# Turning u, v and x by f16 products of their split parts, and a new order in the second scan

## The chip, the cores and the metric

The kernel runs on one core of one Trainium2 chip. The metric is the device time of one execution in microseconds; lower is better. The host prepares arrays (transposes, stacking, repeated rows) but does no arithmetic of the layer.

## The reference, cut to what matters

One layer of a small language model on tokens of shape (2, 2048), model width 192:

```python
h = embed(x) * sqrt(192) + position                  # per token: 192 values
u = rmsnorm(layernorm(h)) * norm1_w
z, xBC, dt = split(u @ in_proj_w)                    # 384, 512, 24 columns
xBC = silu(conv4(xBC) + conv_b)                      # causal, 4 taps
state = exp(dt*A) * state + dt * x * B               # scan over 2048 tokens, 24 heads of 16, 64 states
y = (state . C + D*x) * silu(z)
m = y @ out_proj_w                                   # back to 192
v = rmsnorm(m) * norm2_w
m = m + (silu(v @ w_gate) * (v @ w_up)) @ w_down     # width 768
h = h + m
xn = layernorm(h)
w, idx = route(sigmoid(xn @ gate_weight.T))          # 8 experts in 4 groups, 2 groups, then 2 experts
h = h + shared(xn) + sum of the chosen experts(xn)   # width 128 each
```

## The kernel before, in words

The 2048 tokens are worked in 16 chunks of 128 tokens, both sequences of the batch together (NB = 2), so that most tiles are 128 partitions by 256 tokens. A ramp starts chunks 0 and 1, a body runs 14 times (once unrolled, 13 times in a hardware loop), and a finale ends the last two chunks. One pass of the body works on three chunks at once: `p` (embedding, norm 1, input projection, convolution of the chunk two ahead), `f` (scan of the chunk one ahead) and `b` (output projection, MLP and experts of the oldest chunk). On every engine the order of instructions is written out by hand; engines meet only through semaphores, and each engine takes its own list strictly in order. So an instruction that waits holds up all that is listed behind it on its engine.

Matrix products whose left side is a normalised activation use pairs of f16 numbers: a value is the sum of a high f16 part and a low f16 part. The width of 192 is cut into channels 0 to 127 and the last 64. The last 64 are packed so that one 128-partition tile holds low parts in 64 partitions and high parts in the other 64; weights for them (`wt_hi`, `wt_lo`) stand in SBUF twice, once for each half. One product then takes five matmuls (`split_products`, L1457): three with the first 128 channels and two with the packed 64.

Activations are normalised with tokens on partitions and have to be turned so that channels are on partitions. Before the change that is done in f32: `transpose_channels` (L1466) issues four f32 transposes of 128x128 for one turn (two overlap in 64 channels), for `un` (L1488), `vn` (L1715) and `xn` (L1777). Then ScalarE casts the turned values from PSUM to the high parts (`split`, L642, two instructions) and VectorE subtracts to get the low parts (`split`, L999, two instructions). Only then can the products start.

The part of the body that matters most is the second scan, the scan of sequence 1 of chunk `f`. VectorE's list there (L1437 to L1450) is: `norm2` (add the MLP's result, statistics), `steps_dt` (three small operations for dt of chunk `p`), `masks` 8 and 9, `norm2_apply` (xn, two instructions), `masks` 10 and 11, `from_state` (state's part of y times the decays), `split_x`, `scanned`, `new_state`. A mask (L1115) multiplies a 128x512 tile of exponentials by the masked products of B and C. GpSimd computes 1/sqrt(var) for xn in between (`rsqrt`, L447) and multiplies the scan's state by its decay (`decayed`, L483) as soon as xn is turned (L620). TensorE's list (`second_scan`, L1657, then `experts`, L1821) is: masked 6 and 7, exponents 10, state read, exponents 11, x projection tiles 0 and 1, masked 8 and 9, turn of xn, x projection tiles 2 and 3, masked 10 and 11, then `state_share` (L1695), which overwrites the PSUM bank that `from_state` reads and so waits for it, then the router and the experts.

The first scan (sequence 0) has the same form; there `turn_v` (L1715) comes between `exponents` 6 and `masked` 4, and the MLP's first product waits for v's split.

At the start SyncE issues the loads. Weights go to `w_raw` with one DMA of 128 partitions and to `wt_raw` with two DMAs of 64 partitions, once for the input projection and once for the rest (L340 to L366). GpSimd's `middle_weights` (L576) waits for all of the rest, VectorE's `middle_weights` (L984) waits for GpSimd, and the first masks stand behind it.

Of the kernel before, what the change touches and what calls it, by code (L numbers as in the profile page):

```python
# [29 lines left out]
NB = 2  # L30
# [71 lines left out]
def program(nc, tokens, position, vocab_ids, table, weights, norms, conv_w, conv_b, shared_rows, d_skip, w_out, w_down,  # L102
            w2, identity, lower_ones, triangle_rows, exponent_rows, pair_rows, spread_rows, out):
    with ExitStack() as ctx:
# [3 lines left out]
        def sem(name):  # L108
# [30 lines left out]
        idf = sb("idf", [128, 128])  # L139
        upper = sb("upper", [128, 128])  # L140
# [14 lines left out]
        un = sb("un", [128, NB, D])  # L155
# [47 lines left out]
        vn = sb("vn", [128, NB, D])  # L203
# [10 lines left out]
        xn = sb("xn", [128, NB, D])  # L214
        x_h = sb("x_h", [128, 2, NB * Q], F16)
# [45 lines left out]
        un_ready, ut_done, u_hi_ready, u_hi_tail, u_lo_ready, u_lo_tail = (sem(n) for n in (  # L261
            "un_ready", "ut_done", "u_hi_ready", "u_hi_tail", "u_lo_ready", "u_lo_tail"))
# [32 lines left out]
        m_out, hm_ready, rm_ready, vn_ready, vt_done = (sem(n) for n in (  # L295
            "m_out", "hm_ready", "rm_ready", "vn_ready", "vt_done"))
        v_hi_ready, v_hi_tail, v_lo_ready, v_lo_tail = (sem(n) for n in (
            "v_hi_ready", "v_hi_tail", "v_lo_ready", "v_lo_tail"))
        gu_done, sg_ready, gt_ready = sem("gu_done"), sem("sg_ready"), sem("gt_ready")
        mlp_done, h1_ready, stat2_ready, r2_ready, xnt_done = (sem(n) for n in (  # L300
            "mlp_done", "h1_ready", "stat2_ready", "r2_ready", "xnt_done"))
        xn_ready = [sem(f"xn_ready{b}") for b in range(NB)]
        x_hi_ready, x_hi_tail, x_lo_ready, x_lo_tail = (sem(n) for n in (
            "x_hi_ready", "x_hi_tail", "x_lo_ready", "x_lo_tail"))
# [34 lines left out]
        def _(sp):  # L339
            def load_weights():  # L340

                part = slice(0, COL_G)
                sp.dma_start(w_raw[:, part], weights[0:DH, part]).then_inc(in_w, 16)
                sp.dma_start(wt_raw[0:DT, part], weights[DH:D, part]).then_inc(in_w, 16)
                sp.dma_start(wt_raw[DT:128, part], weights[DH:D, part]).then_inc(in_w, 16)
                sp.dma_start(nrm[:], norms).then_inc(in_w, 16)
# [90 lines left out]
        def _(pool):  # L437
# [121 lines left out]
            def finale(a, b):  # L559
                weighted_x(b, 0)  # L560
                mixed(a)
                pool.wait_ge(vt_done, a + 1)
# [13 lines left out]
            def middle_weights():  # L576
                m = slice(COL_G, COL_E)
                pool.wait_ge(in_w, 64)
                pool.wait_ge(in_mid, 48)
# [26 lines left out]
            def body(p, f, b):  # L606
# [4 lines left out]
                if f is not None:  # L611
                    pool.wait_ge(vt_done, b + 1)
                    decayed(f, 0)
                    keep(f)
                    gate(f, 0)
# [14 lines left out]
        def _(act):  # L630

            act.wait_ge(in_w, 64)
# [5 lines left out]
            act.wait_ge(in_first, 48)  # L638
            for k in range(KT):
                act.activation(skip[:, k], idf[:], ACT.Copy, scale=dsk[:, k:k + 1]).then_inc(setup_a, 1)  # L640

            def split(c, done, src, hi, taken, head, tail):  # L642

                act.wait_ge(done, c + 1)
                if later(c):
                    act.wait_ge(taken[0], c * taken[1])
                act.copy(hi[:, 0, :], src[:, 0:NB * Q]).then_inc(head, 1)
                act.copy(hi[DT:128, 1, :], src[DT:128, NB * Q:2 * NB * Q]).then_inc(tail, 1)
# [109 lines left out]
            def mixed_norm(c, src=p_out[0]):  # L758
                act.wait_ge(rm_ready, c + 1)
                if later(c):  # L760
                    act.wait_ge(vt_done, c)
                for b in range(NB):
                    ins = act.activation(vn[:, b, :], src[:, b * D:(b + 1) * D], ACT.Copy, scale=rm[:, b:b + 1])
                ins.then_inc(vn_ready, 1)

            def swiglu(c, p):
                for f in range(NF):
# [8 lines left out]
                    if f == 4 and p is not None:  # L776
# [9 lines left out]

            def pre_split(c, src=p_misc):
                split(c, ut_done, src, u_h, (z_done[0], 1), u_hi_ready, u_hi_tail)
# [52 lines left out]
            def finale(a, b):  # L841
# [24 lines left out]
                split(b, vt_done, p_y, v_h, (gu_done, NF), v_hi_ready, v_hi_tail)  # L866
# [12 lines left out]
                split(b, xnt_done, p_y, x_h, (h13_done, NX), x_hi_ready, x_hi_tail)  # L879
# [6 lines left out]
            def split_v(b):  # L886
                split(b, vt_done, p_out[1], v_h, (gu_done, NF), v_hi_ready, v_hi_tail)

            def split_x(b):
                split(b, xnt_done, p_out[1], x_h, (h13_done, NX), x_hi_ready, x_hi_tail)  # L890

            def ramp():
                pre_split(0)
                softplus(0)
                for i in range(2):
                    convolved_in(0, i, p_d)
                    first_tap(0, i)
# [50 lines left out]
        def _(ve):  # L948
# [26 lines left out]
            def setup_first():  # L975

                ve.wait_ge(in_w, 64)
                ve.wait_ge(w_in_hi, 2)
                ve.scalar_tensor_tensor(w_lo[:, 0:COL_G], w_raw[:, 0:COL_G], nrm[:, 0:1], w_hi[:, 0:COL_G],
                                        ALU.mult, ALU.subtract).then_inc(w_in_lo, 1)  # L980
                ve.scalar_tensor_tensor(wt_lo[:, 0:COL_G], wt_raw[:, 0:COL_G], nrm[:, 1:2], wt_hi[:, 0:COL_G],
# [17 lines left out]
            def split(c, head, tail, src, hi, lo, lo_ready, lo_tail):  # L999


                ve.wait_ge(head, c + 1)
                ve.wait_ge(tail, c + 1)
# [19 lines left out]
            def pre_stats(c):  # L1023
                ve.wait_ge(h0_ready, c + 1)
                pre_steps.start()
# [9 lines left out]
                ve.bn_aggr(mv[:, 1, :], stat[:, 1, :]).then_inc(stat_ready, 1)  # L1035

            def pre_apply(c):
                ve.wait_ge(r0_ready, c + 1)
                if later(c):
                    ve.wait_ge(ut_done, c)  # L1040
                ve.tensor_scalar(un[:, 0, :], h0_next[:, 0, :], mv[:, 0, 0:1], r0[:, 0:1], ALU.subtract, ALU.mult)
                ve.tensor_scalar(un[:, 1, :], h0_next[:, 1, :], mv[:, 1, 0:1], r0[:, 1:2], ALU.subtract, ALU.mult)\
                    .then_inc(un_ready, 1)

            def pre_split(c, src=p_misc):
                split(c, u_hi_ready, u_hi_tail, src, u_h, u_l, u_lo_ready, u_lo_tail)
# [96 lines left out]
            def mixed(c, src=p_out[0]):  # L1143

                ve.wait_ge(vn_ready, c + 1)
# [6 lines left out]
            def swiglu(c, p, f):  # L1152
                for t in range(NF):

                    ve.wait_ge(sg_ready, c * NF + t + 1)
                    if t == 0:
# [3 lines left out]
                        .then_inc(gt_ready, 1)  # L1160
                    if f is not None and t in (0, 3):
                        masks(f, (6 + t // 3,))
                    if p is not None:
# [3 lines left out]
                        if t == 2:  # L1167
                            pre_apply(p)
                        if t == 4:
                            pre_split(p)  # L1170
# [27 lines left out]
            def norm2_apply(c):  # L1198
                ve.wait_ge(r2_ready, c + 1)
                if later(c):  # L1200
                    ve.wait_ge(xnt_done, c)
                for b in range(NB):
                    ve.tensor_scalar(xn[:, b, :], h1[:, b, :], mv2[:, b, 0:1], r2[:, b:b + 1], ALU.subtract, ALU.mult)\
                        .then_inc(xn_ready[b], 1)
# [109 lines left out]
            def finale(a, b):  # L1314
                masks(b, range(4))
                from_state(b, 0)
                masks(b, (4, 5))
# [21 lines left out]
                hidden(a, 4, p_gu_a)  # L1339
                mixed(b, p_misc)  # L1340
                split(b, v_hi_ready, v_hi_tail, p_y, v_h, v_l, v_lo_ready, v_lo_tail)
# [10 lines left out]
                split(b, x_hi_ready, x_hi_tail, p_y, x_h, x_l, x_lo_ready, x_lo_tail)  # L1352
# [21 lines left out]

            def split_v(b):
                split(b, v_hi_ready, v_hi_tail, p_out[1], v_h, v_l, v_lo_ready, v_lo_tail)

            def split_x(b):
                split(b, x_hi_ready, x_hi_tail, p_out[1], x_h, x_l, x_lo_ready, x_lo_tail)

            def ramp():
# [4 lines left out]
                pre_apply(0)  # L1386
                pre_onehot(1)
                setup_first()
                pre_split(0)
# [4 lines left out]
                pre_apply(1)  # L1394
                for m in range(NM):
                    for k in range(1, KC):
                        convolve_tap(0, m, k)
                operands(0)
                pre_split(1, p_out[1])
# [24 lines left out]
            def body(p, f, b):  # L1424
                if f is not None:
                    masks(f, range(4))
                    from_state(f, 0)
                    masks(f, (4, 5))
# [8 lines left out]
                norm2(b)  # L1437
                if p is not None:
# [17 lines left out]
        def _(pe):  # L1456
# [31 lines left out]
            def pre_turn(c, dst=p_misc):  # L1488
# [591 lines left out]
```

## Time and profile before

| | us |
|---|---|
| median of 3 runs | 842.77 |
| lowest, highest | 842.55, 845.16 |
| the profiled execution's own time | 844.69 |
| its span | 842.9 |

Busy time over the span: PE (TensorE) 794.4 us (94%), DVE (VectorE) 652.8 us (77%), ACT (ScalarE) 538.5 us (64%), POOL (GpSimd) 305.0 us (36%). The page's slices show PE at nine tenths or more from the fifth slice of 40 to the last but one, and a granted TensorE clock of nine tenths or more in all but three of them, which lie in the ramp. Of the chain that ended last, 59% is PE, 17% DVE. The busy share of an engine is an average; which wait ends last is read for each stage from the timeline, which gives the start and the length of each instruction (a row with xN merges N alike; PE's lengths overlap, so for PE the distance of starts counts).

### The profile page before, as it was taken

Reading aid. Unit: us, or ns where it says so; the run is one execution under the profiler, and the core shown is the slowest. Engines: PE = TensorE matmul, PEld = TensorE weight load, DVE = VectorE, ACT = ScalarE, POOL = GpSimd, SP = SyncE. Lnnn points to the kernel's source line nnn. Section 1 sums busy time; section 2 is a strip of 40 time slices with the busy share of each in tenths; the row PEclk is TensorE's granted clock in tenths of the full one; section 3 lists DMA queues with packets and bytes.
Section 4 is the critical chain, followed back from the end, with each engine's and each line's share of the span. In section 5 each row is a group of like instructions: output and inputs, shape, how many; then the busy total and the mean of one; then the engine's idle time right before and its main releaser. Section 6 shows DMA issues by size and latency. Waiting matters only on the chain.

```text
span 842.9 us, 23062 instructions
## 1 busy us (share of the span) xinstructions
PE 794.4 (94%) x7310; PEld 659.0 (78%) x7310; DVE 652.8 (77%) x1680; ACT 538.5 (64%) x1208; POOL 305.0 (36%) x445
## 2 busy tenths in 40 slices
PE   3558999999999999999999999999999999999997
PEld 2435787878888787888878787887878788787786
DVE  5786987977778797877879787787878778787645
ACT  4735575766767576776757667675767767575433
POOL 3552242343424235342423434342343434233222
PEclk9887999999999999999999999999999999999999
DMA  7600000000000000000000000000000000000000
GB/s 252 185 2 14 1 7 20 5 21 0 23 0 5 17 4 19 0 23 0 5 17 5 17 0 23 0 5 17 5 17 0 23 0 5 17 5 10 2 1 19
DMA packets 17107, 16.77 MB, mean 20 GB/s; under 512 B 6322, under 2 KB 15416, under 8 KB 16824
## 3 DMA queue, kind: packets, MB, share of 16 engines
q1 hardware_dynamic: 17080, 16.43, 6.8%
q8 instruction: 15, 0.25, 0.1%
q14 instruction: 12, 0.10, 0.0%
HBM read 12.23 MB, written 4.19 MB: 19 GB/s over the span
## 4 chain that ended last, share of the span: by engine, by line
PE 59%; DVE 17%; issue 11%; POOL 6%; DMA 3%; ACT 2%; DVEq 1%; SPq 1%; POOLq 0%; ACTq 0%
PE bank L1463 24%; PE bank L1744 7%; PE bank L1631 7%; DVE xa L1058 5%; POOL w_raw L555 5%; PE bank L1620 4%; PE bank L1817 4%; PE bank L1700 3%; PE bank L1691 3%; DVE mr L1115 2%; DVE w_raw L1371 2%; PE bank L1676 2%; DMA wt_raw<-weights 2%; DVE w_raw L1284 1%; PE bank L1469 1%
## 5 line engine op out<-in xcount | busy, mean ns | idle before, releaser
L744 ACT ACTIVATE er<-bank 128x512 f32<-128x512 f32 x192 | 109.4, 596 | 57.2 <-PE bank L1620 56.6
L1115 DVE SCALAR_TENSOR_TENSOR mr<-er,gm 128x512 f32<-128x512 f32 x192 | 134.3, 734 | 15.0 <-ACT er L744 14.8
L1817 PE MATMUL bank<-w2t,w_raw 128*128 128x192 f32 x576 | 112.4, 326 | 0.0
L1058 DVE SCALAR_TENSOR_TENSOR xa<-xr,cw_,xa 128x256 f32<-128x256 f32 x192 | 92.8, 492 | 8.8 <-ACT xa L664 7.2
L815 ACT ACTIVATE sg<-bank 128x256 f32<-128x256 f32 x144 | 55.0, 382 | 63.3 <-PE bank L1463 52.4
L1817 PEld LDWEIGHTS bank<-w2t,w_raw 128*128 128x128 f32 x576 | 91.0, 190 | 1.1
L775 ACT ACTIVATE sg<-bank 128x256 f32<-128x256 f32 x90 | 34.5, 383 | 89.3 <-PE bank L1463 89.3
L1631 PE MATMUL bank<-mr,xd 128*32 128x128 f32 x1536 | 71.9, 285 | 15.4 <-DVE mr L1115 14.8
L1463 PE MATMUL bank<-x_h,w_lo 128*128 128x256 f16 x288 | 78.9, 274 | 0.0
L1463 PE MATMUL bank<-x_h,wt_lo 128*128 128x256 f16 x288 | 78.9, 274 | 0.0
L1463 PE MATMUL bank<-x_l,w_hi 128*128 128x256 f16 x288 | 78.9, 274 | 0.0
L1463 PE MATMUL bank<-x_h,wt_hi 128*128 128x256 f16 x288 | 78.9, 274 | 0.0
L1463 PE MATMUL bank<-x_h,w_hi 128*128 128x256 f16 x288 | 78.8, 274 | 0.0
L1744 PE MATMUL bank<-wd,gt 128*128 128x192 f32 x384 | 73.7, 327 | 0.6 <-DVE gt L1159 0.6
L1284 DVE TENSOR_TENSOR w_raw<-sg,bank 128x256 f32<-128x256 f32 x144 | 60.0, 416 | 14.5 <-ACT sg L815 13.6
L451 POOL TENSOR_SCALAR var<-mv 128x2 f32<-128x2 f32 x32 | 6.9, 216 | 175.7 <-DVE mv L1192 127.9
L555 POOL TENSOR_TENSOR w_raw<-w_raw 128x384 f32<-128x384 f32 x64 | 63.9, 998 | 14.6 <-ACT w_raw L803 8.3
L1620 PE MATMUL bank<-ri,lj 128*128 128x512 f16 x192 | 66.6, 385 | 2.6 <-DMA ri<-sums 2.3
L1631 PEld LDWEIGHTS bank<-mr,xd 128*32 128x32 f32 x1536 | 36.2, 110 | 37.1 <-DVE mr L1115 24.1
L1371 DVE SCALAR_TENSOR_TENSOR w_raw<-bank,cw,w_raw 128x192 f32<-128x192 f32 x128 | 47.5, 413 | 19.1 <-POOL w_raw L555 15.4
L1744 PEld LDWEIGHTS bank<-wd,gt 128*128 128x128 f32 x384 | 60.8, 190 | 1.8 <-DVE gt L1159 1.2
L1463 PE MATMUL bank<-v_h,w_hi 128*128 128x256 f16 x192 | 52.3, 273 | 0.8 <-DVE gt L1159 0.3
(240 smaller groups left out, 2169.4 us busy)
## 6 DMA issues: line engine op xcount, KB each, us to landing
out<-w_raw SPq DMA_DIRECT2D x16, 192.0 KB, 2.0
w_raw<-weights SPq DMA_DIRECT2D x1, 1924.0 KB, 10.5
wt_raw<-weights SPq DMA_DIRECT2D x2, 962.0 KB, 15.9
pos<-position SPq DMA_DIRECT2D x16, 96.0 KB, 2.8
ri<-exponent_rows SPq DMA_DIRECT2D x4, 384.0 KB, 4.7
tok<-tokens SPq DMA_DIRECT2D x16, 70.0 KB
sums<-lj SPq DMA_DIRECT2D x16, 64.0 KB, 2.2
ri<-sums SPq DMA_DIRECT2D x64, 12.0 KB
```

What stands on the lines that cost most here:

```text
L555: pool.tensor_tensor(acc[:], acc[:], wt_out[:, e % NWT], ALU.add).then_inc(acc_done, 1)
L744: act.activation(er[:, r % NER], p_d[r % 2][:].rearrange("p (h i) -> p h i", h=HG), ACT.Exp)\
L815: act.activation(sg[:, e % 4, :], src[e][:, 0:NB * Q], ACT.Silu).then_inc(sx_ready, 1)
L1058: ve.scalar_tensor_tensor(xa[:, m], xr[:, m, :, k:k + Q], cw_[:, m, k:k + 1], xa[:, m], ALU.mult, ALU.add)\
L1115: ve.scalar_tensor_tensor(mr[:, r % NER], er[:, r % NER], 1.0, gm[:, r // NQ, :].unsqueeze(1).to_broadcast([128, HG, Q]), ALU.min, ALU.mult)\
L1284: ve.tensor_tensor(hh[:, e % NHH, :], sg[:, e % 4, :], src[e][:, NB * Q:2 * NB * Q], ALU.mult)\
L1371: ins = ve.scalar_tensor_tensor(acc[:, b], p_ex[e][:, b * D:(b + 1) * D], cw[:, b, e - 1:e], acc[:, b], ALU.mult, ALU.add)
L1463: ins = pe.matmul(out_, a, b, start=(i == 0), stop=(i == len(parts) - 1))
L1620: pe.matmul(p_d[r % 2][:].rearrange("p (h i) -> p h i", h=HG), lj[:, b, f, :], ri[:, b, f, of, :], start=True, stop=True).then_inc(d_done, 1)
L1631: ins = pe.matmul(p_y[row:row + 32, k * Q:(k + 1) * Q], xd[:, b, h, :], mr[:, r % NER, heads.index(h), :], start=False, stop=(h % 2 == 1), ...
L1744: ins = pe.matmul(dst[:, b * D:(b + 1) * D], gt[:, f, b * Q:(b + 1) * Q], wd[:, f, :], start=(f == 0 and b == 0), stop=(f == NF - 1), skip ...
L1817: ins = pe.matmul(p_ex[e][:, b * D:(b + 1) * D], hh[:, e % NHH, b * Q:(b + 1) * Q], w2t[:, e, :], start=True, stop=True)
```

## The change

Normalised values are split into f16 parts while tokens are still on partitions, and the parts are turned by f16 matmuls against an f16 identity. `u_t`, `v_t` and `x_t` hold the two parts of each channel side by side (step of two elements). The last 64 channels with both parts are then 128 adjacent columns, and one matmul turns them into the packed tile; its weights are repeated row by row by the host, so that `wt_raw` is loaded by one DMA of 128 partitions. After the turn ScalarE copies the high tile (one instruction) and VectorE the low tile (one instruction).

- u: VectorE subtracts the mean (`uc`, two instructions), ScalarE scales into the high parts (`pre_high`, two instructions, behind its third Silu), VectorE forms the low parts (`pre_low`, two instructions), TensorE turns behind the MLP's last gate and up products instead of the last but one.
- v: ScalarE's scaling writes the high parts in f16, VectorE forms the low parts from PSUM (`v_low`, between masks 4 and 5), TensorE turns behind `exponents` 7.
- x: VectorE does it all: normalise (two instructions), one f16 copy, one subtraction.

```diff
-                ve.tensor_tensor(lo[:], src[:, 0:NB * Q], hi[:, 0, :], ALU.subtract).then_inc(lo_ready, 1)
-                ve.tensor_tensor(hi[0:DT, 1, :], src[DT:128, NB * Q:2 * NB * Q], hi[DT:128, 1, :], ALU.subtract)\
-                    .then_inc(lo_tail, 1)
+            def low_parts(c, src, scale, parts, ready):
+
+                for b in range(NB):
+                    ins = ve.scalar_tensor_tensor(parts[:, b, :, 1], src[b], scale[:, b:b + 1], parts[:, b, :, 0],
+                                                  ALU.mult, ALU.subtract)
+                ins.then_inc(ready, 1)
+
+            def low_in(c, turned, src, lo, ready):
+                ve.wait_ge(turned, c + 1)
+                ve.tensor_copy(lo[:], src).then_inc(ready, 1)
...
             def norm2_apply(c):
                 ve.wait_ge(r2_ready, c + 1)
...
+                ve.wait_ge(xn_ready, c + 1)
+                ve.tensor_copy(x_t[:, :, :, 0], xn[:]).then_inc(xh_ready, 1)
+                ve.wait_ge(xh_ready, c + 1)
+                ve.tensor_tensor(x_t[:, :, :, 1], xn[:], x_t[:, :, :, 0], ALU.subtract).then_inc(xl_ready, 1)
...
                 norm2(b)
+                if f is not None:
+                    masks(f, (8, 9))
+                norm2_apply(b)
                 if p is not None:
                     steps_dt(p)
                 if f is not None:
-                    masks(f, (8, 9))
-                norm2_apply(b)
-                if f is not None:
                     masks(f, (10, 11))
+                split_x(b)
                 if f is not None:
                     from_state(f, 1)
-                split_x(b)
...
-            def transpose_channels(dst, src, done):
-
+            def turn(c, dst, low, parts, high_ready, low_ready, high_turned, low_turned):
+
+                pe.wait_ge(high_ready, c + 1)
                 for b in range(NB):
-                    pe.transpose(dst[:, b * Q:(b + 1) * Q], src[:, b, 0:DH], idf[:])
+                    pe.matmul(dst[:, b * Q:(b + 1) * Q], parts[:, b, 0:DH, 0], id16[:], start=True, stop=True)
+                pe.wait_ge(low_ready, c + 1)
                 for b in range(NB):
-                    ins = pe.transpose(dst[:, (NB + b) * Q:(NB + b + 1) * Q], src[:, b, D - 128:D], idf[:])
-                ins.then_inc(done, 1)
+                    ins = pe.matmul(dst[:, (NB + b) * Q:(NB + b + 1) * Q], parts[:, b, DH:D, :].rearrange("p c s -> p (c s)"), id16[:],
+                                    start=True, stop=True)
+                ins.then_inc(high_turned, 1)
+                for b in range(NB):
+                    ins = pe.matmul(low[:, b * Q:(b + 1) * Q], parts[:, b, 0:DH, 1], id16[:], start=True, stop=True)
+                ins.then_inc(low_turned, 1)
...
                 skipped_x(1, 1)
                 masked(c, (8, 9))
-                turn()
                 if p is not None:
                     project_in_x(p, p_d, (2, 3), c)
+                turn()
                 skipped_x(1, 2)
                 masked(c, (10, 11))
...
-                    pool.wait_ge(xnt_done, b + 1)
+                    pool.wait_ge(xl_turned, b + 1)
                     decayed(f, 1)
...
                 sp.dma_start(w_raw[:, rest], weights[0:DH, rest]).then_inc(in_mid, 16)
-                sp.dma_start(wt_raw[0:DT, rest], weights[DH:D, rest]).then_inc(in_mid, 16)
-                sp.dma_start(wt_raw[DT:128, rest], weights[DH:D, rest]).then_inc(in_mid, 16)
+                sp.dma_start(wt_raw[:, rest], weights[DH:DH + 128, rest]).then_inc(in_mid, 16)
```

## Rows read from the trace of the kernel before

**Rows 1.** Windows: stretch, then busy us and count of each engine, granted clock, DMA.
```profile
450.00:499.00 49.00, 48.73 (x460) 40.73 (x459) 39.41 (x105) 33.38 (x76) 18.23 (x27) 1.00 0.03 10
```
**Rows 2.** Timeline of PE, turn of u: start, length, line, tiles, shape, count.
```profile
436.48 0.38 PE L1469 MATMUL bank<-idf,un 128*128 128x128 f32 x2
436.70 0.38 PE L1471 MATMUL bank<-idf,un 128*128 128x128 f32 x2
```
**Rows 3.** Timeline of PE, f16 products of 128 columns in the running sums.
```profile
455.14 0.22 PE L1583 MATMUL bank<-triangles,pa 128*128 128x128 f16 x1
...
455.25 0.22 PE L1583 MATMUL bank<-triangles,pa 128*128 128x128 f16 x1
```
**Rows 4.** Timeline of PE, the first scan: exponents 6, turn of v, first v product.
```profile
474.52 0.39 PE L1620 MATMUL bank<-ri,lj 128*128 128x512 f16 x1
474.95 0.43 PE L1469 MATMUL bank<-idf,vn 128*128 128x128 f32 x2
...
477.72 0.27 PE L1463 MATMUL bank<-v_h,w_hi 128*128 128x256 f16 x1
```
**Rows 5.** Timeline of DVE, the second scan.
```profile
442.52 0.21 DVE L1071 TENSOR_TENSOR dx<-bank,shared 128x48 f32<-128x48 f32 x1
...
442.98 1.29 DVE L1115 SCALAR_TENSOR_TENSOR mr<-er,gm 128x512 f32<-128x512 f32 x2
444.25 0.67 DVE L1203 TENSOR_SCALAR xn<-h,mv,r 128x192 f32<-128x192 f32 x2
444.83 1.29 DVE L1115 SCALAR_TENSOR_TENSOR mr<-er,gm 128x512 f32<-128x512 f32 x2
446.04 0.55 DVE L1126 TENSOR_TENSOR t<-bank,ecx 128x384 f32<-128x384 f32 x1
446.57 0.42 DVE L1004 TENSOR_TENSOR x_l<-bank,x_h 128x256 f16<-128x256 f32 x1
```
**Rows 6.** Timeline of PE, the same second scan: state share, then the router.
```profile
447.48 0.91 PE L1700 MATMUL bank<-xw,bt 128*128 128x384 f32 x2
448.23 0.17 PE L1463 MATMUL bank<-w_hi,x_h 128*128 128x8 f16 x1
```
**Rows 7.** Timeline of POOL: second scan (two rows), then the first scan's rsqrt.
```profile
443.11 1.11 POOL L453 TENSOR_TENSOR r<-var,mhalf 128x2 f32<-128x2 f32 x1
445.75 1.07 POOL L490 TENSOR_TENSOR state<-state,ends 128x384 f32<-128x384 f32 x1 [1.53 <-PE bank L1785]
...
472.04 0.61 POOL L503 TENSOR_SCALAR vv<-ss 128x2 f32<-128x2 f32 x1 [2.67 <-ACT junk L755]
472.74 1.04 POOL L505 TENSOR_TENSOR rm<-vv,mhalf 128x2 f32<-128x2 f32 x1
```
**Rows 8.** Timeline of DVE: the masks beside these two; in the ramp, masks 6 and 7.
```profile
470.71 2.50 DVE L1115 SCALAR_TENSOR_TENSOR mr<-er,gm 128x512 f32<-128x512 f32 x4
...
51.92 2.08 DVE L1115 SCALAR_TENSOR_TENSOR mr<-er,gm 128x512 f32<-128x512 f32 x2
```
**Rows 9.** Timeline of POOL, the ramp, beside masks 6 and 7.
```profile
52.08 1.38 POOL L497 TENSOR_TENSOR y<-y,zs 128x384 f32<-128x384 f32 x1 [1.89 <-DVE y L1135]
```
**Rows 10.** Groups of DVE: a cast to 16 bits; count, busy us, mean ns, idle before.
```profile
L966 DVE CAST tab<-tab_rest 70x192 bf16<-70x192 f32 x1 | 0.3, 256 | 0.0
```
**Rows 11.** Chain that ended last, in the ramp: start, length, what.
```profile
13.96 17.70 DMA wt_raw<-weights
31.85 4.17 POOL w_hi L581
...
40.82 0.78 DVE mr L1115
```
**Rows 12.** Timeline of ACT, the ramp: the exponentials of masks 0 and 1.
```profile
36.08 1.08 ACT L744 ACTIVATE er<-bank 128x512 f32<-128x512 f32 x2 [1.45 <-PE bank L1620]
```
**Rows 13.** DMA from 12 to 23 us, then from 23 to 32 us.
```profile
DMA packets 853, 4.06 MB, mean 369 GB/s; under 512 B 103, under 2 KB 192, under 8 KB 695
...
DMA packets 403, 1.58 MB, mean 176 GB/s; under 512 B 304, under 2 KB 304, under 8 KB 304
```

More of the change, by code:

```diff
@@ L630, in _ @@
         def _(act):
-            act.wait_ge(in_w, 64)
+            act.wait_ge(in_first, 48)
+            act.copy(id16[:], idf[:]).then_inc(setup_a, 1)
+            act.wait_ge(in_w, 48)
             act.activation(w_hi[:, 0:COL_G], w_raw[:, 0:COL_G], ACT.Copy, scale=nrm[:, 0:1]).then_inc(w_in_hi, 1)
@@ L637, in _, with set_skip, high_in @@
             act.activation(aexp[:], alog, ACT.Exp).then_inc(setup_a, 1)
[L638 to L644, printed above, removed]
+            def set_skip():
+                for k in range(KT):
+                    act.activation(skip[:, k], idf[:], ACT.Copy, scale=dsk[:, k:k + 1]).then_inc(setup_a, 1)
+            def high_in(c, turned, src, hi, taken, ready):
+                act.wait_ge(turned, c + 1)
                 if later(c):
                     act.wait_ge(taken[0], c * taken[1])
-                act.copy(hi[:, 0, :], src[:, 0:NB * Q]).then_inc(head, 1)
-                act.copy(hi[DT:128, 1, :], src[DT:128, NB * Q:2 * NB * Q]).then_inc(tail, 1)
+                act.copy(hi[:], src[:].rearrange("p (k t) -> p k t", k=2)).then_inc(ready, 1)
             def convolved_in(c, i, src=p_d):
@@ L1035, in pre_stats, with pre_low, pre_split @@
                 ve.bn_aggr(mv[:, 1, :], stat[:, 1, :]).then_inc(stat_ready, 1)
-            def pre_apply(c):
-                ve.wait_ge(r0_ready, c + 1)
[L1039 to L1046, printed above, removed]
+                ve.wait_ge(stat_ready, c + 1)
+                for b in range(NB):
+                    ins = ve.tensor_scalar(uc[:, b, :], h0_next[:, b, :], mv[:, b, 0:1], None, ALU.subtract)
+                ins.then_inc(uc_ready, 1)
+            def pre_low(c):
+                ve.wait_ge(uc_ready, c + 1)
+                ve.wait_ge(r0_ready, c + 1)
+                ve.wait_ge(uh_ready, c + 1)
+                low_parts(c, (uc[:, 0, :], uc[:, 1, :]), r0, u_t, ul_ready)
+            def pre_split(c, src=p_out[1][:, NB * Q:2 * NB * Q]):
+                low_in(c, ul_turned, src, u_l, u_lo_ready)
             def convolve_tap(c, m, k):
@@ L1153, in swiglu @@
                 for t in range(NF):
+                    if p is not None and t == NF - 1:
+                        pre_split(p)
                     ve.wait_ge(sg_ready, c * NF + t + 1)
@@ L1160, in swiglu @@
                         .then_inc(gt_ready, 1)
+                    if p is not None and t == 3:
+                        pre_low(p)
                     if f is not None and t in (0, 3):
@@ L1316, in finale @@
                 from_state(b, 0)
-                masks(b, (4, 5))
+                masks(b, (4,))
+                v_low(a)
+                masks(b, (5,))
                 split_v(a)
@@ L1373, in weighed_sum, with v_low @@
                 ins.then_inc(out_sum, 1)
+            def v_low(c, src=p_out[0]):
+                ve.wait_ge(vh_ready, c + 1)
+                low_parts(c, (src[:, 0:D], src[:, D:2 * D]), rm, v_t, vl_ready)
             def split_v(b):
-                split(b, v_hi_ready, v_hi_tail, p_out[1], v_h, v_l, v_lo_ready, v_lo_tail)
+                low_in(b, vl_turned, p_pair[1][:, 0:NB * Q], v_l, v_lo_ready)
             def split_x(b):
-                split(b, x_hi_ready, x_hi_tail, p_out[1], x_h, x_l, x_lo_ready, x_lo_tail)
+                low_in(b, xl_turned, p_out[0][:, NB * Q:2 * NB * Q], x_l, x_lo_ready)
             def ramp():
@@ L1427, in body @@
                     from_state(f, 0)
-                    masks(f, (4, 5))
+                    masks(f, (4,))
+                v_low(b)
+                if f is not None:
+                    masks(f, (5,))
                 split_v(b)
@@ L1486, in pre_embed, with pre_turn @@
                 ins.then_inc(emb_done, 1)
-            def pre_turn(c, dst=p_misc):
-                pe.wait_ge(un_ready, c + 1)
-                transpose_channels(dst, un, ut_done)
+            def pre_turn(c, dst=p_misc, low=p_out[1][:, NB * Q:2 * NB * Q]):
+                if not later(c):
+                    pe.wait_ge(setup_a, 1)
+                turn(c, dst, low, u_t, uh_ready, ul_ready, uh_turned, ul_turned)
             def project_dt(c, dst=p_out[1]):
@@ L1653, in first_scan @@
                 exponents(c, 7)
+                between()
                 masked(c, (5,))
@@ L1767, in swiglu @@
                         exponents(f_, 9)
-                    if f == 4 and p is not None:
+                    if f == NF - 1 and p is not None:
                         pre_turn(p)
```

165 lines of the change are left out of this document (87 added, 78 removed).

## The prediction, made before the changed kernel was run

> **What bounds the kernel now.** I read the page's busy shares first, then one window of the loop, then PE's timeline, and last the lists of DVE and POOL where PE's next wait could come from. In a 49 us window, about one pass of the body, PE is busy for 48.73 us at full granted clock, DVE for 39.41 [rows 1]. So in the 14 passes a microsecond less of PE stream is a microsecond gained, if nothing else is late. What can be late is seen in the second scan. There `from_state` ends at 446.59 and `state_share`, which needs it, starts at 447.48 [rows 5, 6]: DVE has 0.89 us to spare, no more. The times below are those of this one pass. In the ramp another chain sets the end: weights landing, GpSimd, DVE's masks [rows 11].
>
> **PE's stream.** A turn is four f32 transposes; two pairs start 0.22 us apart, so a turn takes 0.44 us [rows 2]. It becomes six f16 products of 128 columns with a weight load each. Such products stand in the running sums, two starts every 0.11 us, so 0.055 us each [rows 3]: 6 x 0.055 = 0.33 us, 0.11 less a turn. Their stationary side is contiguous there; in four of the six new ones it is strided, which no row shows. Bounds: 0.055 us, and the f32 transpose's 0.11 us, by which a turn costs 0.66. I take the f16 row, since load and product overlap in both. The id16 copy happens once, off the path.
> The Trainium skill, "TensorE: Matmul & The Clock Gate", section "Back-to-back issue gap", gives about 81 ns for a sustained pair of weight load and 128-column product. By it a turn would be 0.49 us, slower than now. The rows here disagree (0.055 us with alternating weights), so I go by them; the rule is a rival below.
>
> **The v side.** PE finishes exponents 6 at about 474.74 (0.22 after its start) and begins v's turn at 474.95: 0.2 us lost waiting. The first v product comes at 477.72, behind ACT's two and DVE's two split operations [rows 4]. After the change the turn stands behind exponents 7 and skipped_x, so the high parts are there. DVE's `v_low` (two operations of 192; nearest row xn's pair, 0.67 us, upper bound 0.85 at x_l's 0.42 each [rows 5]) runs while PE does masked 4. Mask 5 is queued behind it, and masked 5 on PE waits some 0.3 us for it. One copy per engine replaces two, so v's first product no longer waits once `state_share` is issued. Net 0.1 from stream and 0.3 from waits: I take -0.4 us, bounds 0 and -0.5.
>
> **The u side.** PE's stream gives -0.11. DVE gets two subtractions, two `low_parts` and a copy for two `un` operations and two split ones; ACT two scalings and a longer copy for two casts. All stand under the MLP's products, whose `gt` tiles are made a full product group ahead; the turn moves behind the last group, and two groups of `mlp_down` hide u's copies. gt 5 stands behind the u copy on DVE, with the same two groups to hide it. Without this cover the copy's 0.4 us would be lost. I take -0.1, so PE reaches the second scan 0.5 us earlier; DVE and POOL, which follow the MLP's end, move along.
>
> **The second scan.** Now follow DVE. After `norm2`, where dx started at 442.52, masks 8 and 9 stand first: 442.52 - 0.5 = 442.02, ending after 1.29 us [rows 5] at 443.31. They now run while POOL computes r2. What that does is seen in the first scan, where four masks run from 470.71 to 473.21 [rows 8]: `vv` takes 0.61 us for two elements, ending with a mask, and `rm` ends at 473.78, 0.57 us after the last mask [rows 7]. POOL's operation waits for a mask to end. So r2 is done at 443.31 + 0.57 = 443.88 and xn starts at 443.91; before, r2 ended at 443.11 + 1.11 = 444.22 [rows 7], xn started at 444.25. Of the 0.5 us gained, 0.34 is left.
> From xn's start, all in DVE's list: xn 0.67; wait 0.03; the f16 copy of 384; wait 0.03; the subtraction of 384; `steps_dt` 0.46 (442.52 to 442.98); masks 10 and 11, 1.21 (444.83 to 446.04); `split_x`, one copy from PSUM, 0.34 (x_l's 0.42 less an overlap of 0.08); `from_state` 0.55 [rows 5]. The subtraction is priced by `from_state`'s 0.55 for 384, 0.47 to the next start. For the copy only a cast of 192 is there, 0.256 us [rows 10]. Bounds for 384: 0.256 (if width cost nothing) and 0.55. I take 0.36: the cast plus 0.10 for 192 more elements, half of what the f32 operations take for as many (0.55 for 384, some 0.35 for one of xn's 192). Sum: 0.67 + 0.03 + 0.36 + 0.03 + 0.47 + 0.46 + 1.21 + 0.34 + 0.55 = 4.12 us, and `state_share` follows 0.05 later: 443.91 + 4.17 = 448.08. Before, xn's start to the end of `from_state` was 2.34 us.
> PE would come there at 447.48 - 0.5 - 0.11 = 446.87. Thus 0.6 us later than before even when nothing collides.
> Something does collide. POOL's `decayed` for sequence 1 is released by x's turn. The low parts end 0.4 us before mask 10 starts; PE has four products left, so POOL begins while mask 10 runs. Such a case stands in the ramp: POOL's `gate` began at 52.08, 0.16 us into mask 6 [rows 9], and masks 6 and 7 took 2.08 us for 1.29 [rows 8]: mask 7 waited for POOL. Before, `decayed` began at 445.75, in mask 11, which had no mask behind it; it ended 0.7 us after that mask's end [rows 5, 7]. So mask 11 is held for about 0.65 us, bounds 0 and 0.79. `split_x`, `from_state`, `state_share` and on PE everything behind stand in that line: 448.73, or 1.2 us later than before a pass (447.48 to 448.7).
> The delay isn't won back: behind `state_share` PE goes on with router and experts without a gap (448.23 is just when the share's 0.75 us is over [rows 6]). ACT's softplus now waits for dt and stands ahead of its x copy; by the same chain that copy is ready some 0.4 us before the router, so it is nearly late, not late. 14 x 1.2 = +16.8 us.
>
> **The ramp.** The last of the weights land at 13.96 + 17.70 = 31.66; POOL's high parts follow, and the first mask starts at 40.82 [rows 11], though its exponentials were begun at 36.08 [rows 12]. Up to 23 us DMA moves 369 GB/s, after that 176, with 1.58 MB left [rows 13]: the two half-height DMAs run at half speed. Full height at 369 GB/s would take 4.3 us for that, not 9, and land 4.4 us earlier. SP also issues two DMAs fewer, and each queue entry behind them moves up. From 40.82 the mask can move up until its exponentials' end near 36.7. I take -3.5, bounds 0 (if the slow stretch isn't due to the height) and -4.4.
>
> **The finale.** Its masks 10 and 11 get copy and subtraction ahead of them (+0.9), and its splits each lose two short operations (about -0.3 a time). I take 0, give or take 1.
>
> **Sum.** 844.69 + 16.8 - 3.5 = 858.0 for the profiled execution, which stands 1.92 above the median of 842.77; so 856 us as median.
>
> **Rivals.**
> - POOL doesn't hold mask 11 (PE's turn comes so late that `decayed` starts after it). For it: only 0.35 us lie between. Then 0.6 x 14 = 8.4, with -3.5 from the ramp: 848.
> - The other side: the second scan's chain stays inside PE's stream, and PE remains the limit. It decides at `state_share`: xn's start to `from_state`'s end would have to take under 2.9 us (443.91 to 446.87) instead of 4.12, say with r2 not held up by masks (-0.6) and copy and subtraction costing next to nothing. For it: PE is 99% busy, so any cover elsewhere pays. Against it: the row prices. The whole 0.6 a pass is kept: 842.8 - 8.4 - 3.5 = 831.
> - The ramp wins nothing, as the loads share one queue whatever their height: 859.6.
> - The 81 ns pair: u and v lose 0.05 instead of gaining 0.11, so 14 x 0.3 = 4.5 more: 860.5. The timeline speaks against it.
>
> **Chances.** Forecast 0.57 (own range 851 to 862), no hold 0.17 (845 to 851), PE stays the limit 0.12, ramp without gain 0.10, the pair rule 0.04. Differences under 0.3% (2.5 us) can't be told from none. Faster gets the 0.12 and a little of the no-hold case's edge, 0.14; same 0.07, from that case with a larger ramp gain; slower 0.79. The range 844 to 864 leaves out the fast case and a tail of further waits in the experts.
>
> **What would show it.** After: f16 turn products 0.055 us apart; first v product about 0.4 us earlier in its pass; DVE idle for half a microsecond before xn; masks 10 and 11 together near 2 us, with `decayed` beside them; PE waiting over 1.5 us before masked 11 and `state_share`; pass length 50.1 instead of 48.9; weights in by about 27.5 us. A `from_state` that ends before PE gets there would make it all wrong.

## The result, and the profile after

The changed kernel takes 865.1 us (median of 6 runs, 863.47 to 867.57), the one before 842.89 beside it on the same chip: a ratio of 1.0259 (95%: 1.0235 to 1.0284). It is slower, as forecast, but by 22 us and not by 13: 865.1 lies above the forecast's range (844 to 864). Below, spans of the two profiled executions are compared: 865.5 us after, 842.9 before. The mean granted clock of the changed kernel's six executions runs from 0.974 to 0.984; the profiled one has 0.974 and took 867.34 us, so it is one of the two longest.

The chain that ended last has one row in each pass that is easy to follow, the last twelve `mlp_down` products (start, length, what). From one to the next is the length of a pass. In the kernel before:

```profile
438.83 1.95 PE bank L1744 x12
...
487.76 1.95 PE bank L1744 x12
```

So 48.93 us. After, the same view:

```profile
246.28 2.02 PE bank L1789 x12
...
298.03 2.02 PE bank L1789 x12
...
449.31 2.02 PE bank L1789 x12
...
499.75 2.02 PE bank L1789 x12
```

Most passes take 50.4 us, 1.5 more than before; but 246.28 to 298.03 is 51.75, and of the 12 passes between the first such row and the thirteenth three are as long as that (51.75 to 51.79).

**The second scan.** The row called h1 below is the one in which `norm2` adds the MLP's result. In the kernel before it is this one on DVE:

```profile
440.91 0.56 DVE L1179 TENSOR_TENSOR h<-bank,hm 128x384 f32<-128x384 f32 x1 [1.21 <-PE bank L1744]
```

The timeline of DVE after, from h1 on (start, length, line, operation, tiles, shape, count, and in brackets the idle time ahead and what ended it), answers to [rows 5]:

```profile
451.45 0.56 DVE L1205 TENSOR_TENSOR h<-bank,hm 128x384 f32<-128x384 f32 x1 [1.35 <-PE bank L1789]
...
453.14 1.29 DVE L1141 SCALAR_TENSOR_TENSOR mr<-er,gm 128x512 f32<-128x512 f32 x2
455.02 0.67 DVE L1229 TENSOR_SCALAR xn<-h,mv,r 128x192 f32<-128x192 f32 x2 [0.58 <-POOL r L452]
455.73 0.39 DVE L1233 CAST x_t<-xn 128x384 f16<-128x384 f32 x1
456.15 0.59 DVE L1235 TENSOR_TENSOR x_t<-xn,x_t 128x384 f16<-128x384 f32 x1
456.63 0.19 DVE L1097 TENSOR_TENSOR dx<-bank,shared 128x48 f32<-128x48 f32 x1
...
457.07 1.93 DVE L1141 SCALAR_TENSOR_TENSOR mr<-er,gm 128x512 f32<-128x512 f32 x2
458.93 0.41 DVE L1027 CAST x_l<-bank 128x256 f16<-128x256 f32 x1
459.26 0.54 DVE L1152 TENSOR_TENSOR t<-bank,ecx 128x384 f32<-128x384 f32 x1
```

The rows show the list that was forecast, in its order: half a microsecond of idling ahead of xn, copy and subtraction, dt, two masks that take 1.93 us where two take 1.29 above, then `split_x` ahead of `from_state`. Beside it POOL, which answers to [rows 7]; its third row runs inside DVE's 1.93 us:

```profile
453.33 0.56 POOL L450 TENSOR_SCALAR var<-mv 128x2 f32<-128x2 f32 x1 [7.53 <-DVE mv L1218]
453.97 1.02 POOL L452 TENSOR_TENSOR r<-var,mhalf 128x2 f32<-128x2 f32 x1
457.55 0.91 POOL L489 TENSOR_TENSOR state<-state,ends 128x384 f32<-128x384 f32 x1 [2.56 <-PE bank L1520]
```

And PE, which answers to [rows 6]:

```profile
457.82 0.42 PE L1677 MATMUL bank<-mr,xd 128*32 128x128 f32 x8
459.06 0.42 PE L1677 MATMUL bank<-mr,xd 128*32 128x128 f32 x8 [0.82 <-DVE mr L1141]
459.91 0.88 PE L1745 MATMUL bank<-xw,bt 128*128 128x384 f32 x2 [0.42 <-issue]
```

PE waits 0.82 us for mask 11, and 0.42 more ahead of `state_share`, which follows `from_state`'s end (459.26 + 0.54) by 0.11. From h1 to `state_share` it is now 459.91 - 451.45 = 8.46 us; before, 447.48 [rows 6] less 440.91 was 6.57.

**The granted clock** is what no forecast had. In windows of PE in a long pass (stretch, its length, busy us and count, granted clock, DMA share, GB/s):

```profile
254.00:256.00 2.00, 1.13 (x16) 1.00 0.00 0
256.00:258.00 2.00, 1.55 (x12) 0.82 0.00 0
258.00:260.00 2.00, 2.00 (x20) 0.50 0.00 0
260.00:262.00 2.00, 2.00 (x17) 0.83 0.00 0
```

PE is not fully busy in 254 to 258, where it has the same waits as those just seen (0.82 us ahead of masked 11, 0.42 ahead of `state_share`); then the clock falls to 0.50, the lower of its two levels (1.2 GHz), and the mean of the next 2 us is 0.83. The pass is 1.33 us longer than its neighbours.

### The profile page after: what moved, and what is told of

The parts are those of the page before. It is cut to its first block, busy times and chain, and to the rows that moved or that the text cites. A ratio compares the mean times of both kernels' runs of the same rounds, so it can differ in the third digit from the quotient of the medians.

```text
span 865.5 us, 23218 instructions
## 1 busy us (share of the span) xinstructions
PE 798.4 (92%) x7406; PEld 659.0 (76%) x7406; DVE 662.2 (77%) x1728; ACT 541.8 (63%) x1193; POOL 301.7 (35%) x445
## 4 chain that ended last, share of the span: by engine, by line
PE 44%; DVE 26%; issue 15%; POOL 9%; ACT 3%; DVEq 1%; DMA 1%; POOLq 0%; SPq 0%; ACTq 0%
PE bank L1506 20%; PE bank L1789 7%; DVE mr L1141 6%; DVE xa L1084 5%; POOL w_raw L554 5%; PE bank L1858 4%; PE bank L1745 3%; PE bank L1677 3%; DVE w_raw L1405 2%; POOL r L452 2%; PE bank L1666 2%; PE bank L1736 1%; DVE w_raw L1315 1%; DVE xn L1229 1%; PE bank L1758 1%
## 5 line engine op out<-in xcount | busy, mean ns | idle before, releaser
L1677 PE MATMUL bank<-mr,xd 128*32 128x128 f32 x1536 | 74.5, 287 | 24.1 <-DVE mr L1141 22.5
L450 POOL TENSOR_SCALAR var<-mv 128x2 f32<-128x2 f32 x32 | 11.7, 365 | 176.1 <-DVE mv L1218 126.8
L496 POOL TENSOR_TENSOR y<-y,zs 128x384 f32<-128x384 f32 x32 | 32.8, 1025 | 59.8 <-DVE y L1161 59.8
```

Of the source, the lines that this page charges most:

```text
L1677: ins = pe.matmul(p_y[row:row + 32, k * Q:(k + 1) * Q], xd[:, b, h, :], mr[:, r % NER, heads.index(h), :], start=False, stop=(h % 2 == 1), ...
```

## The experiments

Ahead of each result stands what was expected of the run: theory A, and rivals B and C with their times. Theory A throughout: DVE's list up to `from_state`, with POOL's operation in it, sets `state_share`, and the PE wait that this makes also lets the clock fall. The rivals were the f16 turns themselves, the u and v parts, ACT's longer list, and a loss in the ramp. Times are ratios to the kernel before, beside which each ran; its median was 844.58 us for the first four and 845.22 for the last three.

**POOL's operation out of the masks.**

```diff
-                    pool.wait_ge(xl_turned, b + 1)
+                    pool.wait_ge(t1_ready[1], f + 1)
                     decayed(f, 1)
```

> The changed kernel, but GpSimd's decay of the state of sequence 1 waits for DVE's weighting (from_state) instead of x's turn, so that it can't begin between DVE's masks 10 and 11. Theory A (the wait before state_share in the second scan is DVE's list, and 0.64 us of it is mask 11 held by GpSimd): masks 10 and 11 take 1.21 to 1.3 us together instead of 1.93, state_share comes 0.6 us earlier, 14 x 0.64 = 9 us less: 856 us, or 852 if the three stretches at half granted clock go too. Rival B (GpSimd's operation is beside the point; copy and subtraction alone hold PE, or the clock sets the time): within 2 us of 865. Rival C (the decay, now later, delays new_state and what stands behind it): 865 to 870.

Measured 853.08 us, ratio 1.0093 (1.0072 to 1.0114), against 1.0259. The timeline of DVE has the two masks, and the chain two passes:

```profile
450.44 1.28 DVE L1141 SCALAR_TENSOR_TENSOR mr<-er,gm 128x512 f32<-128x512 f32 x2
```

```profile
442.68 2.02 PE bank L1789 x12
...
492.48 2.02 PE bank L1789 x12
```

Masks 10 and 11 take 1.28 us, the pass 49.80, 0.63 less. All 12 passes are within 0.06 of that: no long one is left. PE's wait ahead of masked 11 is 0.18 us in it, for 0.82. Theory A holds, 852 to 856; B and C fall.

**dt ahead of masks 8 and 9 again.**

```diff
                 norm2(b)
+                if p is not None:
+                    steps_dt(p)
                 if f is not None:
                     masks(f, (8, 9))
                 norm2_apply(b)
-                if p is not None:
-                    steps_dt(p)
```

> The changed kernel, but DVE takes dt's two operations ahead of masks 8 and 9 again, as before the change. Theory A (DVE's list sets state_share): dt leaves the stretch between xn and state_share (0.46 us), part of it comes back since masks 8 and 9 end 0.46 us later and GpSimd's r2 waits for them; but the decay of sequence 1 now falls in mask 11 and not ahead of it, which frees 0.64 us. 0.6 to 1.2 us a pass less, 14 times: 848 to 857 us. If the pass of the profile loses the PE wait altogether the stretches at half granted clock go as well, some 4 us more. Rival B (the order on DVE is of no account; the f16 turn itself or ACT's longer list holds PE): within 3 us of 865. Rival C (dt ahead delays r2 and xn by its full 0.46 us and the decay still hits a mask): 865.

Measured 843.51 us, ratio 0.9997 (0.9985 to 1.0009), just under A's 848 less the 4 us of the clock that it allowed. B and C fall. One exchange of lines gives back what the change had lost against the kernel before. DVE, then POOL, then the chain:

```profile
441.27 0.67 DVE L1229 TENSOR_SCALAR xn<-h,mv,r 128x192 f32<-128x192 f32 x2
...
442.87 1.28 DVE L1141 SCALAR_TENSOR_TENSOR mr<-er,gm 128x512 f32<-128x512 f32 x2
```

```profile
439.81 0.23 POOL L450 TENSOR_SCALAR var<-mv 128x2 f32<-128x2 f32 x1 [7.52 <-DVE mv L1218]
```

```profile
435.79 2.01 PE bank L1789 x12
...
484.89 2.01 PE bank L1789 x12
```

A pass is 49.10. DVE doesn't idle ahead of xn now: POOL's first operation for r2 (`var`) runs beside dt and takes 0.23 us, where beside mask 8 it took 0.56 above; the second takes 1.11, as before the change; and xn starts 3.34 us after h1 (441.27 - 437.93), where with dt behind it was 3.57. So dt ahead costs nothing, since xn waits for r2 anyway, and dt behind costs its 0.46 and the delay of r2. The two masks take 1.28: x's turn ends later against DVE's list, and POOL starts at 443.71, in mask 11.

**`from_state` ahead of `split_x`**, on top of dt ahead.

```diff
-                split_x(b)
                 if f is not None:
                     from_state(f, 1)
+                split_x(b)
```

> The kernel x2_dt_first with one more exchange on DVE: from_state of sequence 1 ahead of split_x, as before the change. In x2_dt_first PE still waits 0.42 us ahead of state_share, and split_x takes 0.33 us of DVE just ahead of from_state. Theory A (what is left of the loss is DVE's list up to from_state): state_share comes 0.33 us earlier, the pass takes 48.77 us instead of 49.10, the time 843.5 - 14 x 0.33 = 839 us. Rival B (the router, which needs split_x, is then late by as much): 843.5. Rival C (the 0.42 us ahead of state_share is PE's own and not a wait for DVE): 843.5, with the 0.42 us still there.

Measured 840.74 us, ratio 0.9938 (0.9923 to 0.9953). The chain, then PE:

```profile
434.23 2.01 PE bank L1789 x12
...
482.99 2.01 PE bank L1789 x12
```

```profile
443.16 0.88 PE L1745 MATMUL bank<-xw,bt 128*128 128x384 f32 x2
```

The pass is 48.76, 0.34 less, as A had it; the time is 1.7 us above A's 839 and well below the 843.5 of B and C. The timeline lists no wait ahead of `state_share` any more. So the 0.42 us there were a wait for DVE, whatever the releaser's column ("issue") says.

**The high parts of x on ACT**, and DVE's subtraction between masks 10 and 11, on top of that.

```diff
...
+                act.copy(x_t[:, :, :, 0], xn[:]).then_inc(xh_ready, 1)
...
-                ve.tensor_copy(x_t[:, :, :, 0], xn[:]).then_inc(xh_ready, 1)
...
-                    masks(f, (10, 11))
+                    masks(f, (10,))
+                x_low(b)
+                if f is not None:
+                    masks(f, (11,))
...
```

> x5_state_first with the high parts of x copied by ACT, ahead of its softplus, instead of by DVE, and DVE's subtraction between masks 10 and 11. Theory A (a list on DVE that is 0.4 us shorter up to state_share leaves PE no wait, so the f16 turn pays its 0.11 us): a pass of 48.47 us, against 48.58 in x3_x_as_before; 836.7 - 14 x 0.11 = 835 us. Rival B (ACT's copy and the hand-over take longer than DVE's own copy, the low half of the turn waits for it): a pass of 48.8 us or more, 839 us or more. Rival C (the softplus and ACT's later copy of x delay the router): 839 to 842.

Measured 838.71 us, ratio 0.9923 (0.9909 to 0.9937). The chain, then PE:

```profile
433.22 2.01 PE bank L1804 x12
...
481.85 2.01 PE bank L1804 x12
```

```profile
440.55 0.28 PE L1528 MATMUL bank<-id,x_t 128*128 128x128 f16 x2
440.77 0.28 PE L1531 MATMUL bank<-id,x_t 128*128 128x128 f16 x2
```

A pass is 48.63, and the time 838.71 us, between A (48.47, 835) and B (48.8 or more, 839 or more). ACT's copy takes 0.63 us for DVE's 0.39, and DVE's subtraction, behind mask 10, still waits 0.16 us for it; so the second pair of the turn starts 0.22 us after the first, not 0.11. The 0.11 that the f16 turn saves is lost in that wait. C is out: from `state_share` to the experts' first product it is 1.00 us here (441.95 to 442.95), as with x as before.

**x as before, u and v as changed**: the f32 turn of xn, the split behind it, DVE's and PE's order of before in the second scan.

```diff
...
-                turn(c, dst, low, x_t, xh_ready, xl_ready, xh_turned, xl_turned)
+
+                for b in range(NB):
+                    pe.wait_ge(xn_ready[b], c + 1)
+                    pe.transpose(dst[:, b * Q:(b + 1) * Q], xn[:, b, 0:DH], idf[:])
+                    ins = pe.transpose(dst[:, (NB + b) * Q:(NB + b + 1) * Q], xn[:, b, D - 128:D], idf[:])
+                ins.then_inc(xnt_done, 1)
...
```

> The changed kernel with x alone turned as before the change: one f32 turn of xn, the split behind it on ACT and DVE, and the second scan's orders of before on DVE and PE; u and v and the weights' loads stay as changed. Theory A (the whole loss is x's part in the second scan; u and v gain 0.4 us a pass, the ramp 3.5 to 4.5 us): 842.9 - 14 x 0.39 - 4 = 833 to 835 us, faster than both. Rival B (f16 turns as such cost, so that u and v lose too, 0.1 us or more a pass): 843 or more with the ramp's gain. Rival C (only the ramp gains; v's shorter wait is lost in the second scan, where DVE's chain sets the end): 838 to 840.

Measured 836.73 us, ratio 0.9911 (0.9896 to 0.9926): faster than both kernels. It is the lowest ratio of all, though its interval and that of the run just above overlap. The chain:

```profile
430.81 2.01 PE bank L1798 x12
...
479.38 2.01 PE bank L1798 x12
```

48.57 a pass, 0.36 less than before: u's and v's parts gain. By the ratio it is 7.5 us less, a little short of A, which asked for 8 to 10 (842.9 less 833 to 835), and clear of B and C.

**The loads alone**, in the kernel before.

```diff
-                sp.dma_start(wt_raw[0:DT, part], weights[DH:D, part]).then_inc(in_w, 16)
-                sp.dma_start(wt_raw[DT:128, part], weights[DH:D, part]).then_inc(in_w, 16)
+                sp.dma_start(wt_raw[:, part], weights[DH:DH + 128, part]).then_inc(in_w, 16)
...
-                sp.dma_start(wt_raw[0:DT, rest], weights[DH:D, rest]).then_inc(in_mid, 16)
-                sp.dma_start(wt_raw[DT:128, rest], weights[DH:D, rest]).then_inc(in_mid, 16)
+                sp.dma_start(wt_raw[:, rest], weights[DH:DH + 128, rest]).then_inc(in_mid, 16)
...
```

> The kernel before the change with one edit: the last 64 channels of the weights are loaded by DMAs of 128 partitions, one each where there were two of 64. Theory A (the half-height transfers run at half rate, and the ramp's chain from the landing to the first mask is all that this edit moves): weights land 4 to 5 us earlier, the first mask 3.5 us, the time 3.5 to 4.5 us less: 838.5 to 839.5. Rival B (the loads' rate is not due to the height, or the ramp's start is held by something else): 842 to 843. Rival C (the ramp gains, but the first pass gives it back, as the changed kernel's first pass seemed to): 841 to 842.

Measured 840.0 us, ratio 0.9941 (0.9927 to 0.9954): 5 us, a little over A. But the profile says that not all of it is the loads'. The first h1 of the kernel before, then of this one, on DVE:

```profile
98.09 0.55 DVE L1179 TENSOR_TENSOR h<-bank,hm 128x384 f32<-128x384 f32 x1
```

```profile
95.30 0.55 DVE L1177 TENSOR_TENSOR h<-bank,hm 128x384 f32<-128x384 f32 x1
```

2.8 us are won by there, although the first mask starts 4.2 us earlier (36.66 for 40.82 [rows 11]) and the masks that DVE reaches later in the ramp still start 4.5 us earlier (71.30 for 75.78). The rest goes in the products that come next. In windows of PE, the kernel before and then this one:

```profile
74.00:78.00 4.00, 3.27 (x23) 1.00 0.15 42
```

```profile
70.00:74.00 4.00, 3.98 (x12) 0.51 0.14 38
```

The same two groups of output projection run at full clock before and at half clock here: from the exponents just ahead of them to the next skip product it is 4.74 us (70.02 to 74.76), and 2.83 before (74.72 to 77.55). The first pass gives nothing back, 49.20 from h1 to h1 in both, so C is out. The other 1.4 us of the span come in the finale, from the last of the rows followed above to the end, where the clock stayed at 1.00 from 50 to 60 us behind that row (before: 0.84 in those 10 us, with PE as busy, 8.15 us for 8.16). So 2.8 to 4.2 us are the loads', by what the clock does behind them.

**PE kept busy in its wait**, in the changed kernel.

```diff
-                skipped_x(1, 2)
+                for _ in range(4):
+                    skipped_x(1, 2)
                 masked(c, (10, 11))
```

> The changed kernel, with one 128x128 product (the skip product of the last column group in the second scan) made four times instead of once, so that PE works through 0.9 us of the wait ahead of masked 11; the repeats write the same values. Theory A (PE's wait in the second scan is what lets the granted clock fall to half in 3 of the 12 middle passes): no pass at half clock, all at 50.4 to 50.5 us, 3 x 1.33 = 4 us less: 861 us. Rival B (the falls come from elsewhere): 865 with three or so passes of 51.8 us. Rival C (the repeats themselves delay masked 10, masked 11 and state_share): 0.1 to 0.3 us a pass more, 866 to 869.

Measured 862.58 us, ratio 1.0197 (1.018 to 1.0213) against 1.0259. PE, and the chain's first and last of thirteen rows:

```profile
453.31 1.11 PE L1723 MATMUL bank<-xs,skip 128*128 128x128 f32 x8
454.35 0.42 PE L1677 MATMUL bank<-mr,xd 128*32 128x128 f32 x8
455.06 0.43 PE L1677 MATMUL bank<-mr,xd 128*32 128x128 f32 x8 [0.29 <-DVE mr L1141]
455.91 0.88 PE L1746 MATMUL bank<-xw,bt 128*128 128x384 f32 x2 [0.42 <-issue]
```

```profile
142.66 2.02 PE bank L1790 x12
...
747.91 2.02 PE bank L1790 x12
```

(747.91 - 142.66) / 12 = 50.44: work that is of no use shortens the kernel, since no pass is long any more, while `state_share` starts 10.59 us behind the row of its pass (445.32), as in the changed kernel (10.60), so C is out. The repeats filled 0.53 us of the wait (0.29 left of 0.82), not the 0.9 that was expected. The mean granted clock is 0.984 to 0.988 in this kernel's five executions, 0.974 to 0.984 in the six of the changed one. Theory A holds: the falls come from PE's wait.

Together the runs take the pass of the changed kernel apart without a rest that matters (means over the 12 passes of each profile, for the changed kernel over the nine that are not long):

| step | pass, us | worth |
|---|---|---|
| changed kernel | 50.43 | |
| POOL's operation out of the masks | 49.80 | 0.63 |
| instead: dt ahead of masks 8 and 9 (POOL then starts in mask 11 by itself) | 49.11 | 0.69 more |
| and `from_state` ahead of `split_x` | 48.76 | 0.35 |
| and the high parts on ACT | 48.63 | 0.13 |
| x as before, u and v as changed | 48.58 | 0.05 |
| kernel before | 48.93 | -0.35: what u and v gain |

So of the 1.85 us that x's part costs a pass, 1.67 come from the new order in the second scan and from where POOL's operation falls in it. With DVE's order of before, splitting x ahead of its turn costs 0.18 (48.76 for 48.58).

## Why the prediction was right in direction and wrong in size

| term | forecast, us | measured |
|---|---|---|
| 14 passes | 14 x 1.2 = +16.8 | 14 x 1.50 = +21.0 |
| granted clock falls | none | 3 x 1.33 + 1.7 = +5.7 |
| ramp, to the first h1 | -3.5 | 93.77 - 98.09 = -4.3 |
| finale | 0 | +0.2 |
| span | +13.3 | +22.6 |

The 1.7 is the first interval from h1 to h1, 52.4 us for 49.2 before, less 1.5; the granted clock was 0.77 from 101 to 106 us in it, behind the same wait. The finale is from the thirteenth row to the end, 112.27 for 110.54, less one second scan of 1.5.

**The step that failed** is the sum: it has no term for the granted clock, which makes 5.7 of the 9.3 us that are missing, and its largest term is 0.3 a pass too small, another 4.2. The ramp gained 0.8 more than forecast. The clock's term is that of the profiled execution; by the clocks and times on record it differs from execution to execution. The prediction had "PE waiting over 1.5 us" ahead of masked 11 and `state_share` among its signs (it came as 0.82 and 0.42), and had read full granted clock in the loop before [rows 1], where PE is 99% busy; it didn't ask what that clock does once PE waits.

**PE's stream: right.** The timeline after, u's turn:

```profile
448.81 0.27 PE L1513 MATMUL bank<-id,u_t 128*128 128x128 f16 x2
448.92 0.28 PE L1516 MATMUL bank<-id,u_t 128*128 128x128 f16 x2
...
```

A pair every 0.11 us, 0.33 for the three pairs of a turn, for 0.44 [rows 2]; that is 0.055 us a product, as in [rows 3], also with strided weights. The Trainium skill, "TensorE: Matmul & The Clock Gate", section "Back-to-back issue gap", has about 81 ns for such a sustained product with its weight load. The trace does not agree, and the rival that rested on it is out.

**v: right, 0.1 too much.** Exponents 6 and the first v product after, for [rows 4]:

```profile
486.92 0.39 PE L1666 MATMUL bank<-ri,lj 128*128 128x512 f16 x1
...
488.71 0.43 PE L1677 MATMUL bank<-mr,xd 128*32 128x128 f32 x8 [0.17 <-DVE mr L1141]
...
489.81 0.27 PE L1506 MATMUL bank<-v_h,w_hi 128*128 128x256 f16 x1
```

2.89 us for 3.20: -0.31, forecast -0.4. The wait for mask 5 came, 0.17 us for "some 0.3". **u** gave some 0.05 for 0.1: its turn is 0.11 shorter, but the last twelve `mlp_down` products read 2.02 for 1.95 in the chain. Nearly all of that is in the first of them, which now stands right behind the turn: the second starts 0.22 us behind it, for 0.17 before; why, no run tells. Together 0.36, and the run with x as before shows 0.35.

**The second scan: right in each mechanism, a little small in each.** r2 is held behind masks 8 and 9: h1 to xn 3.57 us, forecast 443.91 - 440.41 = 3.50. xn to `state_share` 4.89, forecast 4.17 + 0.65 = 4.82; in it the copy 0.39 (0.36 taken from a cast half as wide), and mask 11 held for 0.63 by the run without POOL (0.65 taken). Those two gaps, the 0.1 that u and v gave less, and the rounding of 1.25 to 1.2 make the 0.3. The hold itself: the masks read `er` and `gm`, POOL's operation reads `state` and `ends`, and the two masks take 1.93 us with it between them, 1.28 without. The Trainium skill, "SBUF — State Buffer", section "Who interferes with whom", says that a Vector instruction with two SBUF inputs contends with a GpSimd one that reads SBUF. The trace agrees. ACT's copy of x was ready at 459.37, ahead of the router at 460.63: nearly late, as forecast, and not late.

**The ramp: right, a bit more.** The weights land earlier and something else is late next. In the timeline of POOL after, for the second row of [rows 11]:

```profile
27.97 0.21 POOL L469 COPY xr<-xr 128x24 f32<-128x24 f32 x1 [4.09 <-DVE xa L1084]
28.18 4.16 POOL L580 TENSOR_SCALAR w_hi<-w_raw,nrm 128x1536 f16<-128x1536 f32 x1
```

The high parts start at 28.18 for 31.85, now behind POOL's small copy `xr`, which waits for DVE's part of the convolution. The first masks start at 37.24 for 40.82, so -3.6 there, and by the first h1 it is -4.3. That 4.3 is one execution's: the runs with POOL's operation out of the masks, with dt ahead and with `from_state` ahead share this ramp, and their first h1 comes at 95.87, 93.73 and 94.61, for 93.77 here. So no run tells the 0.8 above the forecast from the clock's part in the ramp. In the loads-alone run the first masks start 4.2 us earlier. The Trainium skill, "SBUF — State Buffer", section "Can I just issue two DMAs to hit both halves?", says that two transfers of half the partitions run nearly one behind the other and only one over all 128 reaches every port. That run agrees.

**The rivals.** No hold (848): out, POOL did hold mask 11. PE remains the limit (831): out here, but the run with x as before (ratio 0.9911) shows what its condition was worth: u, v and the loads pay, as that rival said, where x's list is not lengthened. Ramp without gain, pair rule: out.

## What to carry to other kernels

Splitting ahead of a turn paid where the parts are ready before PE comes (u, v: 0.35 us a pass) and not where DVE is last to finish (x: 0.18 us a pass lost in DVE's old order, 1.85 in the new one). Before an operation is put into a list, add up the list to the signal that PE waits for, and put work that nobody there waits for into a wait that stands anyway, as dt into the wait for r2. See where GpSimd's operation is released among DVE's two-input ones: between two masks it cost 0.63 us a pass, in the last of them or behind them nothing that the masks show. And when a change makes PE wait in a loop where it didn't, add a term for the granted clock, or fill the wait.

## What the runs showed of the hardware that was not expected

- A wait of PE of 0.82 us, with 0.16 and 0.42 us near it, in a loop otherwise at full clock was followed by a fall of the granted clock to 0.50 in the first pass and 3 of the 12 next, at 1.33 us each for the three; with 0.53 us of the 0.82 filled by products, or with 0.18 in place of the 0.82 (the pass of 49.80 us), in none of the 12. Why these passes and not the others stays open.
- In the ramp the granted clock differs between kernels that start alike: the first output projection ran at 1.00 in the kernel before and at 0.51 with the full-height loads, so 4.5 us won ahead of it were 2.8 at the first h1.
